# Local attention loop of a six-layer transformer kernel: two batches a trip instead of one, the seventh batch written out behind the loop

## The reference

```python
def attn_layer(x, Wqkv, qs, ksc, Wo):            # 16 heads of 64, windows of 32 rows
    q, k, v = split(x @ Wqkv)                     # 128 -> 3 x 1024, in float32
    q, k = l2norm(q) * qs, l2norm(k) * ksc        # per head
    q, k = rotary(q, scale), rotary(k, 1 / scale)
    # each window of 32 queries sees its own 32 keys and the 32 before them
    out = softmax(q @ k2.T * 8 + mask) @ v2
    return out @ Wo
for i in range(6):
    x = attn_layer(shift_tokens(x), ...) + x
    x = ffn_layer(shift_tokens(x), ...) + x       # layer norm, gated GELU, width 341
```

## Time and profile before

| | |
|---|---|
| Median of 3 runs | 5536.82 us (5531.36 to 5545.69) |
| The profiled execution's own time | 5534.48 us |
| Its span, first to last instruction | 5532.5 us |
| Layer 0: first L941 to the end of its last L1020 | 1653.7 to 2181.3 us |
| Six attention parts together | about 3,160 us |
| Mean granted clock of TensorE | 0.907 of full speed |
| Instructions' own DMA queue (q8) | 581 packets of 16 KB |

### The profile page before, as it was taken

How to read it: one execution, slowest core, us unless ns; L and a number is a source line. 1 busy time by engine, 2 the same in 40 slices (tenths; PEclk the granted TensorE clock), 3 DMA queues, 4 the chain that set the end, 5 groups by cost and what they waited for, 6 DMA issues and landing times. The chain is left out here.

```text
span 5532.5 us, 169536 instructions
## 1 busy us (share of the span) xinstructions
PE 4490.3 (81%) x70369; PEld 2832.7 (51%) x70369; DVE 3605.5 (65%) x6107; ACT 2432.7 (44%) x3020; POOL 2513.4 (45%) x3540
## 2 busy tenths in 40 slices
PE   3555666777679998899988999799988999889997
PEld 2333323222226665566655666466665666556664
DVE  6665566665557776677756777576766777567774
ACT  2433433344344444444434444354444454444453
POOL 2000011111137674477626767176653777356771
PEclk9888877788789999999999999899999999999998
DMA  0000000000012222122212222122221222122220
GB/s 27 0 0 0 0 1 0 0 0 0 0 36 68 73 73 56 46 68 69 71 37 65 69 72 71 29 75 69 68 66 38 69 73 71 40 61 70 71 74 16
DMA packets 156862, 247.95 MB, mean 45 GB/s; under 512 B 33488, under 2 KB 50896, under 8 KB 155472
## 3 DMA queue, kind: packets, MB, share of 16 engines
q1 hardware_dynamic: 156240, 238.09, 16.3%
HBM read 20.38 MB, written 2.10 MB: 4 GB/s over the span
## 5 line engine op out<-in xcount | busy, mean ns | idle before, releaser
L1085 ACT ACTIVATE ls_r<-PS 128x1024 f32<-128x1024 f32 x192 | 196.5, 1023 | 1054.8 <-PE PS L963 1054.8
L1164 DVE TENSOR_TENSOR ls_a<-PS,TC 128x1024 f32<-128x1024 f32 x384 | 467.5, 1219 | 171.2 <-ACT ls_r L1085 170.8
L866 POOL TENSOR_TENSOR ls_a<-ls_a,ls_q 128x1024 f32<-128x1024 f32 x192 | 452.9, 2359 | 263.6 <-DVE ls_q L1169 263.6
L1174 DVE TENSOR_REDUCE ls_ss<-ls_r 128x16 f32<-128x1024 f32 x384 | 466.2, 1214 | 86.0 <-ACT ls_r L1110 86.0
L1169 DVE TENSOR_TENSOR ls_q<-PS,TS 128x512 f32<-128x512 f32 x768 | 491.0, 680 | 0.0
L381 POOL TENSOR_TENSOR QT<-MXT,ONE 3x512 bf16<-3x512 bf16 x128 | 146.9, 1148 | 732.7 <-ACT MXT L534 725.5
L886 POOL TENSOR_TENSOR ls_a<-ls_a,ls_q 128x1024 f32<-128x1024 f32 x192 | 455.2, 2371 | 0.0
L963 PE MATMUL PS<-WQ,ls_xsT 128*128 128x512 f32 x768 | 438.8, 700 | 18.4 <-issue 9.7
L1020 PE MATMUL PS<-WO,ls_r 128*128 128x128 f32 x3072 | 404.3, 286 | 58.9 <-ACT ls_r L1113 58.9
L1181 DVE TENSOR_REDUCE ls_mx<-PS 128x8 f32<-128x512 f32 x384 | 263.0, 685 | 246.2 <-PE PS L948 246.2
L1020 PEld LDWEIGHTS PS<-WO,ls_r 128*128 128x128 f32 x3072 | 367.1, 196 | 105.6 <-ACT ls_r L1113 105.6
(11 more groups left out here) (217 smaller groups left out, 9128.2 us busy)
## 6 DMA issues: line engine op xcount, KB each, us to landing
ls_vb<-ls_vt SPq DMA_DIRECT2D x1152, 130.0 KB
ls_vb<-ls_vt SPq DMA_DIRECT2D x672, 65.0 KB
ls_xs<-XL SPq DMA_DIRECT2D x42, 256.0 KB, 2.4
WQ<-wqkv SPq DMA_DIRECT2D x6, 1536.0 KB, 6.5
ls_vb<-ls_vz SPq DMA_DIRECT2D x96, 65.0 KB
WO<-wo SPq DMA_DIRECT2D x24, 128.0 KB, 6.2
X<-x SPq DMA_DIRECT2D x8, 256.0 KB, 5.2
out<-X SPq DMA_DIRECT2D x8, 256.0 KB, 3.5
```

The lines of the kernel that those rows point to most:

```text
L866: pool.tensor_tensor(a4[:, 1], a4[:, 1], b4[:, 1], ALU.add).then_inc(s_ck, 1)
L1164: nc.vector.tensor_tensor(v4(A[fq])[:, a], src, tab, ALU.mult).then_inc(done, 1)
L1174: nc.vector.tensor_reduce(ss[:, fq, a * H:a * H + H], v4(SQ)[:, a], AX.X, ALU.add).then_inc(done, 1)
```

## The change

The body of the loop becomes a function `batch(g)`. The loop runs 3 trips and calls it twice in each, for batches 2p and 2p + 1; batch 6 is written out behind the loop, and batch 7 behind that as before. It holds for all five engines, since all of them get their order from `tiles`. Which slots there are, their order on each engine, their semaphores and their DMAs stay as they are. Seven lines are added near the top, so line numbers below them are 6 higher in the changed kernel's listing (the loop is at line 766).

```diff
-                with eng.Fori(0, B - 1) as g:
+
+                def batch(g):
                     for j in range(NT):
                         front = (g, j + 2) if j < 2 else (g + 1, j - 2)
                         mid = (g, j + 1) if j < 3 else (g + 1, 0)
...
                         if j == 1:
                             prep(g + 1)
+
+                with eng.Fori(0, B // 2 - 1) as pair:
+                    for half in range(2):
+                        batch(pair * 2 + half)
+                batch(B - 2)
                 g = B - 1
```

## The result

| | before | after |
|---|---|---|
| Median of the runs | 5534.09 us (4 runs, 5526.56 to 5545.69) | 5388.66 us (4 runs, 5383.44 to 5400.97) |
| Ratio, 95% interval | | 0.9739 (0.9713 to 0.9765) |
| Span of the profiled execution | 5532.5 us | 5399.2 us |
| Mean granted clock | 0.907 | 0.912 |

Forecast were 5392 us and 0.974 of the time before; measured are 5388.66 and 0.9739. The forecast was put on the scale of three runs of the kernel before (median 5536.82); with the fourth the median is 5534.09, and the gain is 145.4 us against the 145 of the forecast.

A forecast was written before the change was run, and what follows sets the result against it. PE was taken as the bound, stalling at backward jumps; 24 jumps removed at 6.04 us gave 145, so 5534.5 - 145 = 5389.5 us, or 5392 on the runs' scale. Its own range was 5374 to 5410; 8 times in 10, 5374 to 5432.

The forecast's parts named there:

- PE is the bound, and its seams are the weak place: Local attention: PE sets the pace in slots without a branch, but idles and slows its clock behind each backward jump.
- A jump costs 6.04 us, 24 of them 145: Attention loop: each removed backward jump on PE gives back 6.04 us, so 24 of them 145 us.
- A slot without a jump takes 15.31 us there: Slot 0 of a batch, without a jump before it: 15.31 us, read from the last batch behind the loop.
- Idle time and lower clock are both part of it: Of a jump's 6.04 us, 3.63 is idle PE and the remaining 2.4 is work at the lower clock.
- The cause is the fetch of code no longer held: PE's trip has left its instruction memory by the branch, so the jump, 3610 ns on PE, waits for a fetch.
- Nobody needs the stall: No engine uses PE's stall to catch up: POOL has 2.7 us slack a slot; "five slots in a row" ran PE-busy.
- The branches of the others: DVE, ACT, POOL and SP branches, 45 to 56 ns, were taken to cost nothing more with doubled trips.
- rival 3: DVE or ACT begins to miss its branch target in the feed-forward loop: 43 us back, 5432 us; chance 0.07.
- Rival 1: Each removed seam returns only its 3.63 us idle, the clock still falling every batch: 87 us, 5447 us; chance 0.06.
- rival 4: Long-busy PE is held at a lower clock in the attention parts: 5724 us at c = 0.90; chance 0.03.
- rival 2: PE stalls mid-trip as at the branch now, or in every batch anyway: nothing moves, 5534 us; chance 0.04.
- Straight on, the packets come ahead of need: In PE code without a jump, instruction packets arrive in time, so PE stands nowhere for issue.

The follow-up runs named there:

- run 1: Kernel before with two batches a trip on PE alone, the other engines keeping one: ratio 0.974 (0.9705 to 0.9774).
- run 2: Kernel before with two batches a trip on DVE, ACT, POOL and SP, PE keeping one: ratio 1.0002 (0.9984 to 1.0021).
- run 3: Kernel before with half of the scores and half of the weighted-value matmuls left out, PE's trip about 1570 instructions: 5080 us, not comparable.
- run 4: Kernel before with only half of the scores matmuls left out, PE's trip about 2082 instructions: 5470 us.
- run 5: Three batches a trip on every engine, seventh batch written out, six backward jumps in all: 5400.08 us, 0.9737 of the kernel before.
- run 8: Kernel before with 172 semaphore increments on PE, once, ahead of the loop over the layers: 5651.22 us, ratio 1.018.

## Why the prediction was right

- *PE is the bound, and its seams are the weak place.* Right: runs 1 and 2 give PE all of the gain and the others none.
- *A jump costs 6.04 us, 24 of them 145.* Measured 5.95 and 143. The 12 left cost 5.7 each.
- *A slot without a jump takes 15.31 us there.* Measured 15.28 in the mean of 24.
- *Idle time and lower clock are both part of it.* Right: a jump slot at clock 1.00 takes 18.9 us, those shown at 0.84 and 0.85 take 21.6 and 22.6.
- *The cause is the fetch of code no longer held.* Argued from the packets then; shown now by runs 3 and 4, and by PE's going on 2.6 to 3.4 us after a packet's start behind every jump.
- *Nobody needs the stall.* Right: POOL's wait at L881 is 475.6 us in 192 slots, 2.5 each, against the 2.7 of the earlier trace rows.
- *The branches of the others.* Still 45 to 56 ns in the attention loop, DVE's in the feed-forward loop 56 ns; rival 3 is out, and stays out with seven batches written out.
- *Rival 1* (only the idle time goes) fails at the window of 1.00 in the middle of a trip; *rival 4* at the clock of the layers' part (from the first slot to the last), 0.95 before, 0.96 after and 0.97 with all written out; *rival 2* at the seam itself.
- *"Straight on, the packets come ahead of need."* Wrong as a rule, and harmless here by chance. PE had a wait for issue of 1.44 us in straight code in the very trace I read, in the last batch's slot 3, and I passed over it because the stretches I looked at had none. At another place of the code it costs more than jumps save: run 5 lost 44 us to two such stalls and gained 36 by six jumps, and most of the 1.8% by which run 8 was slower is a third stall behind each jump. The changed kernel happens to have no such edge, and has lost the one of slot 3. The forecast had neither in its sum, so being within 0.1% of the time is partly luck; a hit within its range of 18 us either way is what the method can claim.
- *The working.* The sums come out as they stand. One reading does not: "five slots in a row" for the stretch from 2059 to 2116 are 57 us, nearly four slots. What was concluded from it, that no engine needs the stall, held.

What stays open: what decides when a block's packet starts, from 0.8 us ahead of the block's entry to 7.8 us behind it in the rows above, and with it why the third edge behind a jump was caught in run 8 and not in the earlier trace rows; and the 14 us by which the start of the first slot differs between traces of the same early code.

## What to carry to other kernels

Read the loop's compare-and-branch by engine. In this kernel 0.05 to 0.2 us meant that the body was held, and 3.3 to 4.1 us that it was fetched again; then each jump taken cost its idle time and, mostly, a stretch at the lower clock behind it. Only the engine that has this needs longer or written-out trips, and a body short enough to be held is nearly as good (13.96 us for a slot behind a jump in run 3, 13.63 for the next). When code is written out, look for waits "for issue" without a jump ahead of them in a run of short matmuls: five instructions ahead of one took away 21 us here, as much as three or four jumps cost.

## What the runs showed of the hardware

- A backward branch on PE, in the median: 0.21 us (body of 1570 instructions), 0.22 (189), 3.8 (2082), 3.6 (2594). On ACT, DVE, SP and POOL 34 to 73 ns in every run, even where POOL's layer had grown to over 1,000 instructions.
- Behind a jump whose target isn't held PE stands about 2.1 us, and in the kernel before again at the edge of the first block of 256 instructions, 1.5 us in the mean of 36 (0.6 to 1.9); in runs 4 and 8, with the code at another place, for 2.0 to 2.7 us inside the weighted values.
- In straight code an edge that fell 245 to 260 instructions behind the start of the weighted values cost 0.9 to 2.6 us of idle PE (0.3 and 0.6 once each) and 1.3 to 3.8 us for the slot in the mean; an edge 245 to 254 instructions into the scores cost 0.45 us at most where no jump came before.
- Whenever PE stood so inside a slot, it went on 2.2 to 3.1 us after the start of a packet of 16 KB on the instructions' queue.
- The granted clock fell to its lower level behind most of these pauses, and not behind all: jump slots of 18.9 us at 1.00 and 22.6 at 0.85 lie in the same execution.
